# Layer-1 and layer-2/3 attention: two transfers move to the scalar queue, two small splits move from GpSimd to VectorE

## What is computed

```python
for layer in 0..3:
    x = layernorm(x + attention[layer](x))
    x = layernorm(x + ffn[layer](x))
```

```python
d = sqrt(max(|q|^2 + |k|^2 - 2 q.k, 1e-12))      # per head, 256 x 256
p = softmax(-d)                                  # = exp(-(d - min d)) / sum
out = (p @ v).reshape(B, N, 128) @ wo.T + bo
```

## Time and profile before

| | |
|---|---|
| median of 3 runs | 3075.25 us (3058.79 to 3075.34) |
| time of the profiled execution | 3075.25 us |
| its span | 3073.1 us, so 2.15 us lie around it |
| busy over the span | PE 77%, PEld 54%, DVE 50%, ACT 47%, POOL 43% |
| mean granted TensorE clock | 0.857 of full speed |

### The profile page before, as it was taken

One profiled execution on the slowest core, in us unless ns is written; L12 is line 12 of the kernel. 1 busy time (PEld: TensorE's weight loads), 2 busy tenths in 40 slices (PEclk: granted clock), 3 DMA queues, 4 the chain that ended last, 5 costly groups with the idle time before them and its releaser, 6 DMA issues. The chain is left out here.

```text
span 3073.1 us, 51731 instructions
## 1 busy us (share of the span) xinstructions
PE 2372.1 (77%) x17870; PEld 1667.0 (54%) x17870; DVE 1531.9 (50%) x4247; ACT 1430.2 (47%) x3400; POOL 1307.2 (43%) x1807
## 2 busy tenths in 40 slices
PE   6999999982917999872399219999796799966861
PEld 4666666652904555542399204555453577745751
DVE  3555555541136999983133225676102466641653
ACT  4666666650525988860022113677223266522321
POOL 2444444444056877743633542342001333307345
PEclk9999999995955999995699655999898699968985
DMA  3000000002113222102111113231000333111222
GB/s 130 1 1 1 1 1 1 1 2 89 64 41 100 69 63 64 49 3 105 48 49 50 42 54 98 81 90 44 7 0 4 99 101 92 50 38 51 84 66 62
DMA packets 100671, 153.38 MB, mean 50 GB/s; under 512 B 17139, under 2 KB 70277, under 8 KB 93381
## 3 DMA queue, kind: packets, MB, share of 16 engines
q1 hardware_dynamic: 88644, 128.33, 13.6%
q0 software_dynamic: 11776, 21.81, 2.3%
HBM read 99.86 MB, written 48.24 MB: 48 GB/s over the span
## 5 line engine op out<-in xcount | busy, mean ns | idle before, releaser
L830 DVE TENSOR_REDUCE A_nmax<-A_S 128x2 f32<-128x512 f32 (+1 forms) x512 | 309.5, 621 | 238.0 <-PE A_S L658 123.3
L172 POOL TENSOR_SCALAR A_prob<-A_prob,A_rinv 128x256 f32<-128x256 f32 x512 | 236.7, 483 | 355.1 <-DVE A_rinv L388 355.1
L782 ACT ACTIVATE A_PT<-A_E 128x512 f32<-128x512 f32 (+1 forms) x512 | 276.1, 546 | 173.6 <-PE A_E L675 89.9
L1046 POOL TENSOR_TENSOR A_D<-A_D 128x1024 f32<-128x1024 f32 x128 | 239.6, 1896 | 23.3 <-ACT A_D L1240 23.3
L383 DVE TENSOR_REDUCE A_nmax<-A_S 128x2 f32<-128x512 f32 x256 | 164.7, 685 | 154.8 <-PE A_S L259 154.8
L340 ACT ACTIVATE A_prob<-A_S,A_nmax 128x256 f32<-128x256 f32 x512 | 235.1, 478 | 4.9 <-DVE A_nmax L383 4.9
L1634 POOL DMA_INDIRECT sent<-x_state,L_row x160 | 154.2, 964 | 181.8 <-DVEq L1914 133.9
L1654 POOL DMA_INDIRECT L_rows<-results,L_row x160 | 154.8, 967 | 153.8 <-DMA results<-L_ye 108.1
L1313 DVE TENSOR_SCALAR_CACHE_REDUCE A_D<-A_S 128x256 f32<-128x256 f32 x512 | 193.3, 415 | 20.3 <-PE A_S L1121 19.6
L1641 POOL COPY L_wr<-L_w 128x1024 f32 (+1 forms) x144 | 104.4, 727 | 202.8 <-PE L_k L1729 124.4
L1134 PE MATMUL A_T<-ident_sb,A_D 128*128 128x128 f32 x1024 | 163.6, 283 | 30.3 <-DVE A_PT L1319 17.8
(11 more groups left out here) (358 smaller groups left out, 5972.9 us busy)
## 6 DMA issues: line engine op xcount, KB each, us to landing
A_QS<-stack_q SPq DMA_DIRECT2D x144, 192.0 KB
A_KS<-stack_k SPq DMA_DIRECT2D x144, 192.0 KB
L_xe<-sent SPq DMA_DIRECT2D x46, 256.0 KB, 2.9
results<-L_ye SPq DMA_DIRECT2D x46, 256.0 KB, 2.0
stack_q<-A_parts SPq DMA_DIRECT2D x48, 192.0 KB, 2.1
stack_k<-A_parts SPq DMA_DIRECT2D x48, 192.0 KB, 2.3
L_w<-f_w SPq DMA_DIRECT2D x24, 256.0 KB
sent<-A_zeros SPq DMA_DIRECT2D x9, 512.0 KB
```

What stands on the lines that cost most here:

```text
L172: nc.gpsimd.tensor_scalar(prob[:, n % NP, j, t, :], prob[:, n % NP, j, t, :], rinv[:, n % NP, j, t:t + 1], 1.0, ALU.mult, ALU.mult).then_i ...
L782: nc.scalar.activation(PT[:, n % RING, :], psE[n % 2][:, 0:BLOCKS, :].rearrange("p a b -> p (a b)"), ACT.Exp, scale=scale).then_inc(expd, 1)
L830: nc.vector.tensor_reduce(nmax[:, b % 2, :, h], view, AX.X, ALU.max, negate=True).then_inc(maxed, 1)
L1046: nc.gpsimd.tensor_tensor(d3, d3, m, ALU.subtract).then_inc(less_min, 1)
```

## The change

In `attention_small` POOL's `send_max` is gone. ACT's `take_max` waits for its own copy to be written and issues the transfer itself; before the copy it now waits for the transfer of the batch before (it was the one before that). In `attention_dist` SP's `lengths` is gone in the same way: `take_lengths` on ACT issues both transfers, and takes over SP's wait that the buffer is free. POOL's `split_rest` is gone: its two instructions stand at the end of `split_lengths` on DVE. The rest drops a switch that was always on (`BY_POOL` held all eight units, so `take_min` and `exps` run as before).

```diff
 # attention_small
-                def send_max(b):
-                    pool.wait_ge(nm_ready, b + 1)
-                    after(pool, nm_in, 16 * b)
-                    pool.dma_start(QS[ROWS:RUN, b % NBUF, :, :], nmT[:, b % 2, :]).then_inc(nm_in, 16)
...
                 def take_max(b):
                     act.wait_ge(nm_psum, b + 1)
-                    after(act, nm_in, 16 * (b - 1))
+                    after(act, nm_in, 16 * b)
                     nc.scalar.activation(nmT[:, b % 2, :], ..., ACT.Copy).then_inc(nm_ready, 1)
+                    act.wait_ge(nm_ready, b + 1)
+                    act.dma_start(QS[ROWS:RUN, b % NBUF, :, :], nmT[:, b % 2, :]).then_inc(nm_in, 16)
 # attention_dist
-                def lengths(b):
-                    sp.wait_ge(n2t_ready, b + 1)
-                    after(sp, n2_in, 32 * b)
-                    after(sp, scored, H * (b - NBUF + 1))
-                    sp.dma_start(QS[CROSS:CROSS + PARTS, b % NBUF, :, :], n2T[:, b % 2, 0:SEQ]).then_inc(n2_in, 16)
-                    sp.dma_start(KS[CROSS + PARTS:KR, b % NBUF, :, :], n2T[:, b % 2, SEQ:]).then_inc(n2_in, 16)
...
-                def split_rest(b):
-                    pool.wait_ge(n2_split, 4 * b + 2)
-                    nc.gpsimd.tensor_copy(n2p[:, :, 1, :], n2r[:]).then_inc(n2_split, 1)
-                    pool.wait_ge(n2_split, 4 * b + 3)
-                    nc.gpsimd.tensor_tensor(n2p[:, :, 2, :], n2r[:], n2p[:, :, 1, :], ALU.subtract).then_inc(n2_split, 1)
...
                 def take_lengths(b):
                     act.wait_ge(n2t_psum, b + 1)
-                    after(act, n2_in, 32 * (b - 1))
+                    after(act, n2_in, 32 * b)
+                    after(act, scored, H * (b - NBUF + 1))
                     nc.scalar.activation(n2T[:, b % 2, :], ..., ACT.Copy).then_inc(n2t_ready, 1)
+                    act.wait_ge(n2t_ready, b + 1)
+                    act.dma_start(QS[CROSS:CROSS + PARTS, b % NBUF, :, :], n2T[:, b % 2, 0:SEQ]).then_inc(n2_in, 16)
+                    act.dma_start(KS[CROSS + PARTS:KR, b % NBUF, :, :], n2T[:, b % 2, SEQ:]).then_inc(n2_in, 16)
...
                 def split_lengths(b):
                     nc.vector.tensor_copy(n2p[:, :, 0, :], n2).then_inc(n2_split, 1)
                     dve.wait_ge(n2_split, 4 * b + 1)
                     nc.vector.tensor_tensor(n2r[:], n2, n2p[:, :, 0, :], ALU.subtract).then_inc(n2_split, 1)
+                    dve.wait_ge(n2_split, 4 * b + 2)
+                    nc.vector.tensor_copy(n2p[:, :, 1, :], n2r[:]).then_inc(n2_split, 1)
+                    dve.wait_ge(n2_split, 4 * b + 3)
+                    nc.vector.tensor_tensor(n2p[:, :, 2, :], n2r[:], n2p[:, :, 1, :], ALU.subtract).then_inc(n2_split, 1)
```

More of the change, by code:

```diff
@@ L618, in _ @@
                         split_max(b)
-                    if (b := at(s, NM_AT + 1)) is not None:
-                        send_max(b)
                     if (b := at(s, OT_AT - 4)) is not None:
@@ L887, in attention_dist @@
     BY_SCALAR = ()
-    BY_POOL = tuple(range(U))
     SLOTS = NB * H
@@ L1013, in _ @@
                         stack(b)
-                    if (b := at(s, N2T_AT + 1)) is not None:
-                        lengths(b)
             @block.gpsimd
@@ L1062, in _ @@
                         split_qk(b)
-                    if (b := at(s, N2_AT + 2)) is not None:
-                        split_rest(b)
-                    if (u := unit(s, SUB_AT)) is not None and u % U in BY_POOL:
+                    if (u := unit(s, SUB_AT)) is not None:
                         take_min(u)
@@ L1242, in exps @@
                 def exps(u):
[L1243 to L1251, removed]
+                    act.wait_ge(less_min, u + 1)
+                    nc.scalar.activation(D[:, u % RD, 0:W], D[:, u % RD, 0:W], ACT.Exp, scale=-1.0).then_inc(expd, 1)
                 def take_turned(n):
```

## The result

| | before | after |
|---|---|---|
| median | 3075.3 us | 3107.8 us |
| span of the profiled execution | 3073.1 us | 3103.4 us |
| attn1, first transpose to last `write_x` | 918.1 to 1377.6: 459.5 us | 918.0 to 1423.0: 505.0 us |
| nine rounds of attn1, from `write_x` to `write_x` | 233.74 us, 25.97 each | 261.15 us, 29.02 each |
| attn2, ffn2 and attn3, taken the same way | 1820.1 to 2713.9: 893.8 us | 1865.2 to 2747.4: 882.2 us |

The changed kernel takes 1.0125 times as long (95% interval 1.0106 to 1.0143). Attn1 became 45.5 us longer, the stretch from attn2 to attn3 11.6 us shorter. Of the 45.5 us, 15.5 are lost before the first `write_x`, while the pipeline fills (117.2 us before, 132.8 after), 27.4 in the nine rounds, and 2.5 behind them.

What follows compares the result with a forecast made beforehand. DVE was taken to bound attn1 (98% busy), PE attn2 and attn3. Split 34.6, lengths on ACT 1.8, clock 3.3, send_max 3.0, less 1.0, gave 41.7 us on 3075.25: 3117 us, range 3074 to 3136.

Steps and rivals of the forecast that it cites:

- The new pair: attn1, DVE: the added cast and subtraction wait for POOL's take_min, 2.8 us a round, 34.6 us in all.
- Only the cast is shut out: Rival, attn1: the subtraction is not held off, the pair costs 1.4 us a round, 3098 us in all; chance 16%.
- The two engines shut each other out: attn1, write_x beside POOL: DVE and POOL block each other for whole instructions; the pair takes 2.79 or 2.80 us a round.
- The filling: attn1's start: batches 0 and 1 cost nothing, 2 and 3 cost 0.5 us each, 12 later batches the full price.
- I count no gain: attn1, write_x: a later split_qk could cut it from 2.8 to about 1.8 us, but DVE would wait for late transposes.
- DVE at 98%: attn1, sign expected in the new profile: DVE still 98% busy, with rounds 28.5 to 29 us long.
- The clock: attn1: three more falls to the lower clock at 1.1 us each, 3.3 us; bounds 0 and 13.
- +3.0-1.0 us: attn2 and attn3: late exponentials cost 0.1 us for 30 batches, 3 us; earlier first transfers of a step gain 1 us.
- unchanged within 5 us each: attn2 and attn3, sign: neither moves by more than 5 us; time moving there would show the prediction wrong.
- Late ACT: Rival, attn1: ACT's longer issues or surviving lateness hit DVE in full, another 11 to 19 us, 3132 us; chance 12%.
- The passing pair: Rival, attn1: POOL does not hold off DVE's new instructions, write_x shortens, about 3073 us; 11% together with no effect.
- the change without effect: Rival: POOL's idle time and the transfers were hidden anyway, DVE's instructions free, 3075 us; 11% together with the passing pair.

Runs made afterwards that it cites:

- after_again: The whole change unchanged, measured a second time beside other runs, against the kernel before: ratio 1.0165, attn1 509.5 us.
- split_alone: The kernel before with only split_rest's two instructions moved from POOL to the end of split_lengths on DVE: ratio 1.0156, attn1 511.0 us.
- lengths_alone: The kernel before with only take_lengths on ACT issuing both transfers in place of SP: ratio 1.0009, attn1 457.7 us.
- writex_pool: The kernel before with only attn1's write_x moved from DVE to POOL, behind root_var: ratio 0.9938, attn1 437.4 us.
- rows_alone: The kernel before with only the attention_small edit, take_max on ACT issuing the transfer in place of POOL's send_max: ratio 1.0017, attn1 459.4 us.
- writex_lengths: The kernel before with attn1's write_x on POOL and the lengths' transfers issued by ACT: ratio 0.9989, attn1 454.0 us.

## Why the prediction came out as it did

**The median, 3107.8 for 3117 predicted.** The direction and the mechanism of attn1 were those predicted. That the number is so near is in part luck: attn1 lost 45.5 us for 39.7 predicted, attn2 to attn3 gained 11.6 where +2.0 was predicted, most of that gain comes from a stretch at the lower clock that no run ties to the change, and the second measurement of the same kernel, 1.0165, would be 3126 us.

**The new pair: right.** Predicted 2.8 us a round from the earlier trace rows, measured 2.43, and 2.82 in after_again. What is shut out is as described, instruction by instruction. The step-by-step reading from the earlier trace rows had given 3.1 us, and split_alone, where nothing else shifts, measured 3.08. In the whole change the cast sometimes comes just before a `take_min` ends, as at 1203.43. "Only the cast is shut out" is refuted: from the fourth batch on it is the subtraction that is always caught. "The two engines shut each other out" says more than the traces show: only DVE's instructions become longer. The 128 `take_min` of attn1 take 1892 to 1903 ns before and 1885 to 1903 after.

**The filling: counted too low.** The prediction gave the third and the fourth batch 0.5 us each and let the full prices begin with the fifth. The pair was caught from the third on (1.93, 2.85, 2.56 and 2.50 us for the third to the sixth batch), and ACT's issues were not hidden there. The fill lost 15.5 us, of which my terms cover 7 to 8. Run alone, the split loses 10.1 us in the fill and the lengths on ACT 4.8.

**"I count no gain" at `write_x`: half right.** I had 2.8 going to 1.8, and with ACT's issues alone it does (1.79 in lengths_alone). In the whole change it went further, to 0.95 us in the round shown, because `split_qk` waits for `take_qk` by up to 1.7 us and POOL is then in its shorter instructions. Over the nine rounds that is 25.15 to 9.19 us of DVE. But DVE did then stand in front of late work, as the step said, and my price for that, 0.15 us a round, was far too low. DVE's idle time grew by 18.6 us in the nine rounds, 2.1 us each. The two together come close to zero, and so the term left out did little harm. In lengths_alone the gain at `write_x` is larger than the loss, 0.50 us a round, and the fill takes it back.

**DVE at 98%: wrong.** I expected DVE still full. It is at 239.60/261.15 = 92%. With its stalls moved and PE late behind ACT, the round is no longer DVE's alone; DVE and PE wait for each other in turn.

**The clock: too low a count.** I added three falls; there are 17 where 5 were (19 on the other chip), about two a round. Priced by my own 1.1 us that is 13 us, the upper bound I gave. The nine rounds give a second reading: the same 1766 matmuls keep PE busy 221.63 us in place of 210.73, 10.9 us more. Part of it is within the waits of the point before, so the two must not be added. The time at the lower clock goes with the stalls of DVE: 79 us in split_alone, 38 and 48 where the pair is short, 3 in writex_pool, where `write_x` is gone from DVE as well. No run changes the clock alone, so its share is not isolated.

**The sum of attn1.** 34.6+1.8+3.3 = 39.7 us was predicted there; 45.5 us came, and 50.0 in after_again. What the sum lacks is in the fill, 8 us; the rounds came out some 2 us cheaper than their part of it.

**Attn2 and attn3: wrong in three places.** I had +3.0-1.0 us and "unchanged within 5 us each", and named a move there as a sign of being wrong; attn2 moved by 14.9 us and attn3 by 5.0. In attn3's steady state nothing changed: eight rounds take 142.24 us before (2479.59 to 2621.83) and 142.29 after (2511.92 to 2654.21), so the 0.1 us a batch for late exponentials was 0. In attn2 it was 0.39: eight rounds take 138.93 us before and 142.02 after, both without a fall of the clock.

```profile
1955.80:2094.73 138.93, 134.22 (x1235) 80.20 (x1232) 102.04 (x217) 98.22 (x217) 53.62 (x96) 1.00 0.33 94
```

```profile
1981.62:2123.64 142.02, 135.94 (x1233) 79.80 (x1232) 102.08 (x218) 97.43 (x218) 48.35 (x88) 1.00 0.31 92
```

In these eight rounds of the kernel after, PE's weight load waits once a round for an exponential; in those of the kernel before there is no such wait:

```profile
PEld A_E L671 <- ACT A_PT L775: 3.6, 8, 0.7
```

The eight rounds are 141.8 to 142.0 us in all eight kernels with this edit and 138.9 to 139.0 in the six without. The first batch, for which I had counted 1 us gained, loses. Who waited for `nmT` at the start of attn3 (2411 to 2512 us) in the kernel after:

```profile
  PEld A_E L665: 3.0, 1
  PE A_E L665: 2.6, 1
```

PE's weight load waits 3.0 us for the first transfer here and 3.7 us in attn2, 3.1 and 3.8 us in rows_alone; before it waited once, 1.3 us, in attn2. The transfer is issued no later (45.6 us into attn3 before, 45.6 after), and it lands later: in attn3 its packets in the trace run from 1.7 to 5.2 us behind the issue before, from 4.1 to 8.6 us after. In the trace it now runs on a hardware queue as SP's 192 KB transfers do, where POOL's ran on a software queue. In the ninth batch either kind is through 1.9 us behind its issue. That the transfer stands behind SP's is the likely cause, and was not tried. Over all profiled runs attn3 takes 330.6 to 333.2 us in the six kernels without this edit and 335.3 to 336.8 in the eight with it.

The largest part, with the other sign, is a stretch at the lower clock that runs from the end of ffn1 into attn2, just over 0.5 in both kernels:

```profile
1726.00:1941.00 215.00, 100.07 (x498) 51.88 (x499) 87.73 (x241) 55.78 (x126) 95.64 (x119) 0.53 0.24 67
```

```profile
1772.00:1936.00 164.00, 47.44 (x226) 24.25 (x226) 65.89 (x202) 32.48 (x78) 81.20 (x95) 0.54 0.23 67
```

It lasts 215 us before and 164 after, and attn2 takes 349.6 and 334.7 us. Sorted by its length, attn2 takes 337 to 338 us at 184 to 188 us of it without the edit and 342.5 to 345.4 at 181 to 188 with it; at 215 to 218 us it takes 349.5 without and 357 with. So at a like stretch the edit costs attn2 5 to 7 us (3.1 in the eight rounds and 2.4 at the first transfer are most of it), and a stretch 51 us shorter gave some 20 us back. Of the six kernels without the edit none had a stretch under 184 us, of the eight with it three had 164. Whether the edit makes the short one more frequent stays open. By the ratio, in which all of it is contained, rows_alone comes to +0.17% (-0.04 to +0.38).

**Late ACT.** Given 12%, at 11 to 19 us. In attn1's rounds it did not happen, for the reason given (others waited first): lengths_alone has shorter rounds than the kernel before. In the fill it cost 4.8 us, in attn2 0.39 us a round. writex_lengths shows what it costs attn1 where DVE is not full: 16.6 us.

**The passing pair and the change without effect** are refuted by the durations of L1280 and L1282.

One slip: the text before calls `write_x` slot 8 of the round; it is slot 7. No number hangs on it.

## What to carry to other kernels

Before moving a small elementwise step from GpSimd to VectorE, look where its inputs lie and what GpSimd will be doing then: an idle gap of GpSimd that ends on VectorE may be the only moment at which the two don't collide, and a value kept in PSUM costs VectorE its own 0.22 us where the same value in SBUF cost up to 1.85. A single instruction whose longest run is several times its shortest, like `write_x`, is the sign to look for, and moving it (0.6% here) was the gain. A transfer issued by a computing engine is free only while something else is later than that engine: here it was free in attn1's full rounds, and not in the filling, in attn2, or once `write_x` had left VectorE. Measure it again whenever the bound moves, and look at the filling apart from the steady rounds: a third of attn1's loss was there.

## What the runs showed that I had not expected

- A transfer issued on ACT blocks it 0.73 us (median 729 ns in each of the three places, 64 in all), as one on SP does, and two behind a copy delay the next activation by 1.57 us.
- A `tensor_scalar` on 128x128 values takes 0.80 us on POOL (777 to 804 ns over 32) and 0.34 us on DVE when nothing is in its way; yet POOL was the better place.
- The added lateness of one engine can shorten another's work: ACT 1.57 us late took `write_x` from 2.79 to 1.79 us, and together with the new pair to 0.95 us in most rounds.
- The stretch at the lower clock at the beginning of attn2 lasted from 164 to 218 us in kernels that differ little or not at all there, and about 0.4 us of attn2 hang on each microsecond of it (15+5 us for 51).
- The 24 KB transfer issued by ACT landed later in the first batch than the same one issued by POOL, 8.6 us behind its issue and not 5.2: PE's weight load waited 3.0 us for it in attn3, where it had not waited before.
- Only VectorE's instructions became longer where it met GpSimd; `take_min` kept its 1.9 us throughout.
